# A top-32 cross-attention on one core: the rest rows of two batches share one tile

## The chip, the cores and the metric

The kernel runs on one core of a Trainium2 chip. The metric is the device time of one execution in microseconds (us). A difference under about 0.3% can't be told from none.

## The reference

The input x is 16 batches of 100 rows of 512 numbers, the context 16 batches of 722 rows. One decoder layer is computed: three sublayers, each added to x.

```python
x = x + self_attn(layernorm(x))      # 4 branches of 16 heads, masks by distance, one learned null key per head
x = x + cross_attn(layernorm(x), ctx, ctx)
x = x + real(ifft(fft(layernorm(x)) @ w)) + bias

# cross_attn, 16 heads of 32 dims:
scores = q @ k.T / SCALE                     # 16 x 16 x 100 x 722
top_scores, top_idx = top_k(scores, 32)
w = softmax(top_scores)
out = (w @ take(v, top_idx)) @ Wo.T + bo
```

## The kernel before

It is two programs, one after the other. The first (`self_program`) does the self-attention for all batches and writes its sum to DRAM, the second (`cross_program`) the cross-attention and the feed-forward product. Each loops over the batches, all five engines run one instruction stream each, written out by hand, and semaphores order them. Factors of matrix products are split into a high and a low part and multiplied in three products (`split3`, L86 to L90).

**The second program.** The queries of one batch have 16 heads x 100 rows. Four heads share a group of 32-dimension strips, so a group has 4 x 100 = 400 query rows: three tiles of 128 rows and 16 rows left over. Four groups make 12 full tiles, and the 4 x 16 = 64 rows left over are tile 12, the rest tile (`Tile.rest`). Since its rows belong to four groups, it needs keys and queries gathered from partitions 96 to 127 of each group: `rest_keys` and `rest_queries` (SyncE, L1014 to L1032) copy them with eight and four DMAs into `RKH`, `RKL` and `R32`. `RKH` and `RKL` lie in the memory of `raw`, into which `load_context` loads the next batch's context.

A batch is seven steps (`STEPS`), six with two full tiles and the seventh with the rest tile. For each tile TensorE makes 128 x 722 scores in `pS` (`score`), ScalarE copies them to `S` (`keep_scores`, L1426), and VectorE finds the 32 greatest of each row in four rounds: MAX8 finds eight, MATCH_REPLACE8 replaces them by a very small number in `W` (L1604, L1613, L1621, L1624). It does the rounds of the step's two tiles in turns. ScalarE exponentiates `S` and `W`, GpSimd subtracts (`weights`, L1102), which leaves the weights of the 32 chosen keys, TensorE transposes them (`weights_T`, L1255) and multiplies with the values (`values`, or `rest_values` for the rest tile), ScalarE copies numerators and denominators to `NR`, and GpSimd, or VectorE for the rest rows (L1633), multiplies them into `ctxT`.

The streams are staggered by steps (`tiles_at`): in step s VectorE works on `cur`, TensorE scores the tiles `coming` next and transposes and multiplies the `old` ones of two steps before, ScalarE and GpSimd treat the `last` ones. Three pairs of buffers `S` and two of `W` hold this. Beside it, TensorE projects the keys and values of the next batch in 14 slices, placed by the table `PLAN`: for each step, slices before and after the second scores.

```python
    PLAN = [([12], [13]), ([], [0, 1]), ([2], [3]), ([4, 5], [6]), ([], [7, 8, 9]), ([10], []), ([], [11])]
```

Step 0 in the list is for the batch's own last two slices. Slice 10 is the last key slice. Also in the steps: the next batch's queries in step 1, the last batch's output projection in step 2 (L1348), its feed-forward product in step 5 (L1321). The high part of the queries (`QH`) is made by ScalarE and the low part (`QL`, `query_low`, L1135) by GpSimd in step 5. Each batch's first tile waits for both.

**The first program.** In the stretch before batch 0 the weights stream in through nine buffers in the memory of `E`; ScalarE makes the high parts, VectorE the low parts of 16 pieces (`lows`, L458) and GpSimd those of the 8 value pieces (`v_low`, L302). The null key's rows, one for the weights in `E` and one for the values in `V`, are made in partition 0 and copied by DMA to partition 100 (`nulls`).

## Time and profile before

| | |
|---|---|
| median of 3 runs | 2210.67 us (2207.01 to 2215.05) |
| the profiled execution | 2211.0 us |
| its span in the trace | 2209.2 us |
| first program | about 0 to 680 us |
| second program: first search on VectorE, last | 735.0 us, 2174.5 us |

The page gives for each engine the time in which it was busy. "Idle before" is the time in which an engine stood still ahead of a group of instructions, with the engine and line that ended it. L is a line of the kernel. In the order of time, a line merges neighbours of one kind ("x6"), with the start, the duration of all together and in brackets the idle time ahead. Operations of VectorE overlap somewhat, so a sum of durations is more than the time they take. PEclk is TensorE's granted clock as a share of 2.4 GHz.

### The profile page before, as it was taken

The numbers are of one execution on the slowest core, as the hardware profiler recorded it, in microseconds if no ns is written. First come the engines' busy times: TensorE is split into PE (matmuls) and PEld (weight loads), VectorE is DVE, ScalarE is ACT, GpSimd is POOL, SyncE is SP. The second block draws the span as 40 slices with busy tenths as digits, with TensorE's granted clock in tenths as the row PEclk, the third lists the DMA queues.
The fourth block names the chain that finished last, engine by engine and source line by source line (L and its number), as shares of the span: only waits on it lengthen the run. The fifth ranks groups of instructions, "written<-read, shape, count | busy, mean of one in ns | idle before, by whom it ended". The sixth has DMA issues, their size and how long they took to land.

```text
span 2209.2 us, 50184 instructions
## 1 busy us (share of the span) xinstructions
PE 1969.3 (89%) x19536; PEld 1531.8 (69%) x19536; DVE 1886.3 (85%) x3501; ACT 1325.0 (60%) x2640; POOL 1297.0 (59%) x1566
## 2 busy tenths in 40 slices
PE   4899999999988889999898998998989989899866
PEld 2566666666563778787787777886878777777753
DVE  6667576767644699999999999999999999999993
ACT  4333333333322577877777778787777777777753
POOL 6465565656443356666656656666565666666542
PEclk8899999999988999999999999999999999999976
DMA  6000000000036010111101101111010110110100
GB/s 199 13 16 21 16 16 21 13 24 13 24 143 145 28 36 14 41 31 36 33 21 53 33 21 41 27 40 33 22 53 19 36 39 21 48 33 22 36 1 12
DMA packets 51175, 82.35 MB, mean 37 GB/s; under 512 B 9809, under 2 KB 26465, under 8 KB 50938
## 3 DMA queue, kind: packets, MB, share of 16 engines
q1 hardware_dynamic: 46442, 71.70, 11.1%
q0 software_dynamic: 2736, 4.16, 1.0%
q10 hardware_dynamic: 1760, 3.28, 0.5%
q8 instruction: 155, 2.54, 0.5%
q14 instruction: 82, 0.67, 0.1%
HBM read 60.54 MB, written 9.86 MB: 32 GB/s over the span
## 4 chain that ended last, share of the span: by engine, by line
DVE 44%; PE 10%; issue 9%; ACT 3%; POOL 1%; DMA 1%; POOLq 0%; DVEq 0%; ACTq 0%; another core or an unknown queue 0%
DVE ca_top L1613 19%; DVE ca_W L1624 17%; DVE ca_W L1621 4%; DVE ca_top L1604 3%; PE ca_pF L88 2%; PE ca_pF L89 2%; PE ca_pF L90 2%; DMA x_scratch<-y_scratch 1%; PE ca_pX L1357 1%; ACT ca_W L1409 1%; PE ca_pT L1255 1%; PE ca_pO L1302 1%; PE ca_pS L88 1%; PE ca_pX L1348 1%; POOL ca_S L1102 0%
## 5 line engine op out<-in xcount | busy, mean ns | idle before, releaser
L1624 DVE MATCH_REPLACE8 ca_W<-ca_top,ca_W 128x722 f32<-128x722 f32 (+1 forms) x624 | 555.1, 899 | 0.0
L1613 DVE MAX8 ca_top<-ca_W 128x8 f32<-128x722 f32 (+1 forms) x624 | 538.5, 903 | 1.7
L1102 POOL TENSOR_TENSOR ca_S<-ca_S,ca_W 128x722 f32<-128x722 f32 (+1 forms) x208 | 357.8, 1740 | 104.5 <-ACT ca_W L1409 104.5
L88 PE MATMUL ca_pS<-ca_KH,ca_QH 128*128 128x362 f32 (+1 forms) x384 | 150.5, 392 | 105.7 <-ACT ca_S L1426 97.8
L1080 POOL TENSOR_TENSOR ca_KL<-ca_K,ca_KH 128x384 fp32r<-128x384 f32 (+1 forms) x128 | 123.0, 961 | 200.8 <-ACT ca_KH L1401 198.3
L1419 ACT ACTIVATE ca_S<-ca_S,ca_shift 128x722 f32<-128x722 f32 (+1 forms) x208 | 175.9, 891 | 54.2 <-POOL ca_shift L1094 54.0
L1409 ACT ACTIVATE ca_W<-ca_W,ca_shift 128x722 f32<-128x722 f32 (+1 forms) x208 | 186.5, 897 | 27.4 <-DVE ca_W L1624 27.2
L341 POOL TENSOR_TENSOR sa_ss<-sa_ss,sa_minus_half 100x16 f32<-100x16 f32 x64 | 190.1, 2986 | 21.2 <-DVE sa_ss L528 21.2
L1431 ACT ACTIVATE ca_PT<-ca_pT 128x768 f32<-128x768 f32 (+1 forms) x208 | 163.0, 784 | 65.4 <-PE ca_pT L1255 61.1
L88 PE MATMUL ca_pF<-ca_cH,ca_WkH 128*128 128x338 f32 (+1 forms) x512 | 188.5, 368 | 9.4 <-ACT ca_K L1399 9.4
L1604 DVE MAX8 ca_top<-ca_S 128x8 f32<-128x722 f32 (+1 forms) x208 | 180.0, 903 | 16.6 <-ACT ca_S L1426 16.2
L1426 ACT ACTIVATE ca_S<-ca_pS 128x722 f32<-128x722 f32 (+1 forms) x208 | 159.7, 768 | 56.1 <-PE ca_pS L90 55.7
L1621 DVE MATCH_REPLACE8 ca_W<-ca_top,ca_S 128x722 f32<-128x722 f32 (+1 forms) x208 | 184.8, 897 | 0.0
L1088 POOL TENSOR_TENSOR ca_cL<-ca_raw,ca_cH 128x768 fp32r<-128x768 f32 (+1 forms) x60 | 103.0, 1738 | 137.5 <-ACT ca_cH L1386 137.5
L438 ACT ACTIVATE sa_E<-sa_pq 100x300 f32<-100x300 f32 x256 | 86.5, 426 | 157.9 <-PE sa_pq L90 157.8
L1255 PE MATMUL ca_pT<-ca_ident,ca_S 128*128 128x128 f32 (+1 forms) x1248 | 176.2, 278 | 4.5 <-ACT ca_PT L1431 3.7
L89 PE MATMUL ca_pF<-ca_cL,ca_WkH 128*128 128x338 f32 (+1 forms) x512 | 174.3, 340 | 0.0
L90 PE MATMUL ca_pF<-ca_cH,ca_WkL 128*128 128x338 f32 (+1 forms) x512 | 173.5, 339 | 0.0
L519 DVE TENSOR_TENSOR sa_qk<-sa_pp,sa_bias_qk 100x512 f32<-100x512 f32 x64 | 44.3, 691 | 141.4 <-PE sa_pp L90 141.4
L88 PEld LDWEIGHTS ca_pS<-ca_KH,ca_QH 128*128 128x128 f32 x384 | 76.2, 199 | 125.3 <-ACT ca_S L1426 110.0
L1255 PEld LDWEIGHTS ca_pT<-ca_ident,ca_S 128*128 128x128 f32 (+1 forms) x1248 | 140.3, 144 | 26.4 <-issue 15.7
L330 POOL TENSOR_SCALAR_AFFINE_SELECT sa_E<-sa_E 100x400 f32<-100x400 f32 x256 | 146.9, 574 | 17.9
(223 smaller groups left out, 5142.1 us busy)
## 6 DMA issues: line engine op xcount, KB each, us to landing
ca_raw<-in_ctxT SPq DMA_DIRECT2D x32, 384.0 KB, 3.7
ca_raw<-in_ctxT SPq DMA_DIRECT2D x32, 338.0 KB, 3.1
ca_RKH<-ca_KH SPq DMA_DIRECT2D x64, 90.2 KB, 2.1
ca_RKL<-ca_KL SPq DMA_DIRECT2D x64, 90.2 KB, 2.1
sa_xin<-in_x SPq DMA_DIRECT2D x16, 200.0 KB
sa_xres<-in_x SPq DMA_DIRECT2D x16, 200.0 KB
x_scratch<-sa_x SPq DMA_DIRECT2D x16, 200.0 KB
x_scratch<-y_scratch POOLq DMA_DIRECT2D x16, 200.0 KB, 13.6
```

The source lines that it names most:

```text
L88: pe.matmul(out, ah, bh, start=start, stop=False)
L89: pe.matmul(out, ah, bl, start=False, stop=False)
L90: return pe.matmul(out, al, bh, start=False, stop=stop)
L341: pool.tensor_tensor(part, part, minus_half[:, 0:NH], ALU.pow).then_inc(norm_ready, 1)
L1102: pool.tensor_tensor(S[k][rows, :], S[k][rows, :], W[r][rows, :], ALU.subtract).then_inc(p_ready, 1)
L1255: last = pe.transpose(pT[:, 128 * k:128 * k + t.rows], S[slot(tb, t)][0:t.rows, KEY0[k]:KEY0[k] + 128], ident[0:t.rows, 0:t.rows])
L1409: act.activation(W[r][rows, :], W[r][rows, :], ACT.Exp, bias=shift[rows, r:r + 1], scale=SCALE).then_inc(f_ready, 1)
L1419: act.activation(S[slot(tb, t)][rows, :], S[slot(tb, t)][rows, :], ACT.Exp, bias=shift[rows, r:r + 1], scale=SCALE).then_inc(e_ready, 1)
L1604: dve.max(top[r][rows, 0:8], S[slot(tb, t)][rows, :]).then_inc(peaked, 1)
L1613: n_of[t.i] = order.mark(dve.max(top[r][rows, 8 * k:8 * k + 8], W[r][rows, :]))
L1621: dve.match_replace(W[r][rows, :], eight, S[slot(tb, t)][rows, :], REMOVED).then_inc(removed, 1)
L1624: ins = dve.match_replace(W[r][rows, :], eight, W[r][rows, :], REMOVED)
```

## The change

**The second program.** The rest tiles of batches 2n and 2n+1 become one tile of 128 rows, which is the seventh step of the even batch; an odd batch has six steps. Rows 0 to 63 are the even batch's, 64 to 127 the odd one's. TensorE makes the scores of each half by itself (`score` and `rest_score`, both in step 5 of the even batch), ScalarE copies the second to partitions 64 to 127 of `S`. There is still one pair `RKH`, `RKL`: SyncE copies the odd batch's keys into it once the first half is scored, and the next context load waits for the second half's scores. The gathered queries have two buffers now, and are made a batch ahead. The last key slice of an odd batch is projected in step 4 of the even one (`PAIR_PLAN`). In an odd batch the next batch's query parts are made in step 4 and its first scores come after the feed-forward product (`swap`). The output of the second half goes to `second_rest`, and in the next batch's step 2 ScalarE copies it to `ctxT`.

**The first program.** VectorE makes the low parts of all 24 pieces; `v_low` is gone. The null rows are made in partitions 96 to 100, of which the values overwrite the first four, so the two copies go. GpSimd issues the small loads first and the biases after the first four high parts.

```diff
+            for t, a in SETUP:
+                pool.dma_start(t, a).then_inc(setup_in, 16)
...
-            def v_low(u):
...
+                    need(pool, null_values, n)
+                    pool.tensor_tensor(V[null, n, :], V[null, n, :], null_bias[n], ALU.subtract).then_inc(null_values, 1)
                 pool.wait_ge(null_values, NL)
-                pool.dma_start(V[T:T + 1, :, :].rearrange("p n d -> p (n d)"),
-                               V[0:1, :, :].rearrange("p n d -> p (n d)")).then_inc(null_in, 16)
-                pool.wait_ge(null_weights, 1)
-                pool.dma_start(E[T:T + 1, :, :, :].rearrange("p h n q -> p (h n q)"),
-                               E[0:1, :, :, :].rearrange("p h n q -> p (h n q)")).then_inc(null_in, 16)
...
+                    pool.wait_ge(hi_made, CC)
+                    for t, a in BIAS:
+                        pool.dma_start(t, a).then_inc(bias_in, 16)
+                    nulls()
...
-                    for u in range(QKU, QKU + CC):
-                        v_low(u)
...
                     biased(2)
+                    lows(range(QKU, QKU + 2))
                     squares(2)
+                    biased(3)
+                    lows(range(QKU + 2, QKU + CC))
+                    squares(3)
                     rope(0)
-                    biased(3)
-                    squares(3)
+                    lows(range(QKU + CC, len(UNITS)))
+                    rope(1)
                     statistics(1)
-                    rope(1)
                     summed()
                     rope(2)
                     rope(3)
                     normalised(1)
+                    picks()
                     order.finish()
...
+    RUN = [(b, s) for b in range(B) for s in range(7 - b % 2)]
+    PLACE = [(b, t.i) for b, s in RUN for t in STEPS[s]]
...
+    PAIR_PLAN = [([12], [13]), ([], [0, 1]), ([2], [3]), ([4, 5], [6]), ([7], [8, 9, 10]), ([], []), ([11], [])]
...
+        R32 = [sb(f"R32{p}", [128, 4 * REST]) for p in range(2)]
+        RH, RL = ([sb(f"{n}{p}", [128, 4 * REST], F32R) for p in range(2)] for n in ("RH", "RL"))
...
+        NR = sb("NR", [128, 2, PAIR])
+        second_rest = sb("second_rest", [128, 4 * REST])[3 * DH:128, :]
...
+        def ring(b, t):
+
+            return 2 * (step_of(b, t) % 2) + t.i % 2
...
+            if tiles and s == 6 and b.const % 2:
+                return [], [], [], [], []
+            at = RUN.index((b.const, s)) if tiles else (s - 7 if b.const < 0 else len(RUN) + s)
+
+            def of(n):
+                if not 0 <= n < len(RUN):
+                    return []
+                ob, os = RUN[n]
+                return [(At(ob), ob % 2, t) for t in STEPS[os]]
+
+            return of(at), of(at - 1), of(at - 2), of(at + 1), of(at - 3)
...
+            return (PAIR_PLAN if b.const % 2 else PLAN) if b.const else FIRST_PLAN
...
+            def rest_keys(b, p, after):
+
+                need(sp, s_mm, after)
                 sp.wait_ge(k_hi, b.count(8, 8))
                 sp.wait_ge(k_lo, b.count(8, 8))
-                for to, of in ((RKH, KH[par]), (RKL, KL[par])):
+                for to, of in ((RKH, KH[p]), (RKL, KL[p])):
                     for g in range(4):
-                        sp.dma_start(to[DH * g:DH * g + DH, :].bitcast(F32), of[3 * DH:128, g, :].bitcast(F32)).then_inc(rk_in, 16)
+                        sp.dma_start(to[DH * g:DH * g + DH, :].bitcast(F32),
+                                     of[3 * DH:128, g, :].bitcast(F32)).then_inc(rk_in, 16)
...
+                if tiles and b.const % 2:
+                    rest_keys(b, par, scored(b.next(-1), NT))
+                    sp.wait_ge(s_mm, scored(b, 0))
...
+                    rest_queries(b.next(), 1 - par)
+                if tiles and not b.const % 2:
+                    sp.wait_ge(ctx_hi, b.next().count(4, 4))
+                    sp.wait_ge(ctx_lo, b.next().count(4, 4))
+                    rest_keys(b, par, scored(b, 0))
...
-                    if s == 5 and tiles and nxt:
+                    if s == 5 and tiles and nxt and not b.const % 2:
                         query_low(bn)
                     for x in first + second:
                         if slice_of(x[0], x[2])[1] == "K":
                             key_low(*x)
-                    if s == 2 and tiles:
-                        pool.wait_ge(r_hi, b.count(1, 1))
-                        pool.tensor_tensor(RL[:, :], R32[:, :], RH[:, :].bitcast(F32), ALU.subtract).then_inc(r_lo, 1)
                     if s == 0 and nxt:
                         pool.wait_ge(squares1_ready, bn.count(1, 1))
                         scales(rstd1_ready)
                     if s == 3 and prev:
                         pool.wait_ge(squares2_ready, b.count(1, 0))
                         scales(rstd2_ready)
+                    if s == 4 and nxt:
+                        rest_query_low(bn, pn)
                     if s in (0, 3) and tiles and nxt:
                         for piece in range(2):
                             context_low(bn, 2 * (s // 3) + piece)
+                    if s == 4 and tiles and nxt and b.const % 2:
+                        query_low(bn)
...
+            def rest_score(tb, p, before):
+
+                pe.wait_ge(r_lo, tb.count(1, 1))
+                pe.wait_ge(rk_in, tb.count(128, 128))
+                pe.wait_ge(s_ready, before)
+                for keys, cols in KEYS:
+                    last = split3(pe, pS[0:4 * REST, cols], RH[p][:, :], RL[p][:, :], RKH[:, keys], RKL[:, keys], True, True)
+                last.then_inc(s_mm, 1)
...
+                pe.wait_ge(kv_out, tb.next().count(NSL, NSL))
+                pe.matmul(pO[3 * DH:128, DEN:DEN + PAIR], rZ[:, r:r + 1].broadcast_to((128, DH)), ident[:, :],
                           start=True, stop=True)
-                for g in range(4):
-                    at = NUM + REST * g
-                    for k in range(KC):
-                        last = pe.matmul(pO[3 * DH:128, at:at + REST], V[tp][:, k, 128 * g + 3 * DH:128 * g + 128],
-                                         PT[t.i % 2][:, k, REST * g:REST * g + REST], start=k == 0, stop=k == KC - 1)
+                for p in (tp, 1 - tp):
+                    for g in range(4):
+                        at = 4 * REST * p + REST * g
+                        for k in range(KC):
+                            last = pe.matmul(pO[3 * DH:128, NUM + at:NUM + at + REST],
+                                             V[p][:, k, 128 * g + 3 * DH:128 * g + 128],
+                                             PT[0][:, k, at:at + REST], start=k == 0, stop=k == KC - 1)
...
+                    swap = s == 5 and tiles and b.const % 2
+                    if coming and not swap:
...
+                    if coming and swap:
+                        score(*coming[0])
...
+                    if s == 5 and tiles and not b.const % 2:
+                        rest_score(bn, 1 - par, scored(b, NT))
...
+            def keep_second_rest(tb, tp, t):
+                act.wait_ge(s_mm, scored(tb, NT + 1))
+                act.activation(S[slot(tb, t)][4 * REST:128, :], scores[0:4 * REST, :], ACT.Copy).then_inc(s_ready, 1)
...
+                    if s == 2 and prev and not b.const % 2:
+                        act.wait_ge(ot_ready, b.count(GROUPS, -1))
+                        act.wait_ge(second_ready, b.const // 2)
+                        act.activation(ctxT[3 * DH:128, :, T - REST:T], chunks(second_rest, 4), ACT.Copy).then_inc(ot_ready, 1)
...
+                        dve.max(top[r][:, 0:8], S[slot(tb, t)][:, :]).then_inc(peaked, 1)
...
-                        if k == 3 and s == 1 and prev:
+                        if k == 3 and s == 1 and prev and b.const % 2:
                             dve.wait_ge(ot_ready, b.count(GROUPS, -1))
-                            dve.wait_ge(o_kept, b.count(GROUPS, 0))
-                            rest = [chunks(NR[3 * DH:128, i, 0:4 * REST], 4) for i in range(2)]
-                            dve.tensor_tensor(ctxT[3 * DH:128, :, T - REST:T], rest[0], rest[1],
+                            dve.wait_ge(o_kept, kept(b, 0))
+                            rest = [chunks(NR[3 * DH:128, i, :], 8) for i in range(2)]
+                            dve.tensor_tensor(ctxT[3 * DH:128, :, T - REST:T], rest[0][:, 0:4, :], rest[1][:, 0:4, :],
                                               ALU.mult).then_inc(ot_ready, 1)
+                            dve.tensor_tensor(chunks(second_rest, 4), rest[0][:, 4:8, :], rest[1][:, 4:8, :],
+                                              ALU.mult).then_inc(second_ready, 1)
                         if k == 1 and s == 3 and tiles and not prev:
```

On TensorE, in step 5 of batch 2: the feed-forward product (`ca_M`), the last key slice (`ca_cH`, `ca_WkH`), the rest tile's scores (`ca_RKH`), the transposes (`ca_ident`, `ca_S`). Before:

```order
L88 MATMUL ca_pS<-ca_RKH,ca_RH 64x362 [waits ca_s_ready,ca_rk_in,ca_r_lo]
...
L1321 MATMUL ca_pX<-ca_M,ca_xT 100x512 [waits ca_x2T_ready]
L1321 MATMUL ca_pX<-ca_M,ca_xT 100x512 x3
L1323 MATMUL ca_pX<-ca_x,ca_ident 100x512 [waits ca_x2f_ready]
L88 MATMUL ca_pF<-ca_cH,ca_WkH 128x338 [waits ca_kv_out]
...
L1255 MATMUL ca_pT<-ca_ident,ca_S 128x128 [waits ca_pt_ready,ca_p_ready]
L1255 MATMUL ca_pT<-ca_ident,ca_S 128x128 x5
L1297 MATMUL ca_pO<-ca_ident,ca_rZ 32x100 [waits ca_rz_ready,ca_pt_ready,ca_o_kept]
```

And after:

```order
L88 MATMUL ca_pS<-ca_RKH,ca_RH 64x362 [waits ca_s_ready,ca_rk_in,ca_r_lo]
...
L1352 MATMUL ca_pX<-ca_M,ca_xT 100x512 [waits ca_x2T_ready]
L1352 MATMUL ca_pX<-ca_M,ca_xT 100x512 x3
L1354 MATMUL ca_pX<-ca_x,ca_ident 100x512 [waits ca_x2f_ready]
L1282 MATMUL ca_pT<-ca_ident,ca_S 128x128 [waits ca_pt_ready,ca_p_ready]
L1282 MATMUL ca_pT<-ca_ident,ca_S 128x128 x5
L88 MATMUL ca_pS<-ca_RKH,ca_RH 64x362 [waits ca_s_ready,ca_rk_in,ca_r_lo]
...
L1327 MATMUL ca_pO<-ca_ident,ca_rZ 32x100 [waits ca_rz_ready,ca_pt_ready,ca_o_kept]
```

The key slice is gone from this step, and a second group of scores from gathered keys stands ahead of the values.

On SyncE's queue, from the even batch's keys to the next context load. Before:

```order
L1032 DMA ca_RKH<-ca_KH 32x722 [waits ca_k_hi,ca_k_lo,ca_ctx_lo,ca_ctx_hi]
L1032 DMA ca_RKH<-ca_KH 32x722 x3
L1032 DMA ca_RKL<-ca_KL 32x722 x4
L1044 DMA ca_xin<-x_scratch 100x512 [waits ca_x2T_mm,ca_x1T_mm]
L1020 DMA ca_R<-ca_qT 32x16 [waits ca_q_ready,ca_s_mm,ca_zeroed]
L1020 DMA ca_R<-ca_qT 32x16 x3
L1012 DMA ca_raw<-in_ctxT 128x2x384 [waits ca_ctx_lo,ca_ctx_hi] x2
```

And after:

```order
L1043 DMA ca_RKH<-ca_KH 32x722 [waits ca_k_hi,ca_s_mm,ca_k_lo,ca_ctx_lo,ca_ctx_hi]
L1043 DMA ca_RKH<-ca_KH 32x722 x3
L1043 DMA ca_RKL<-ca_KL 32x722 x4
L1056 DMA ca_xin<-x_scratch 100x512 [waits ca_x2T_mm,ca_x1T_mm]
L1043 DMA ca_RKH<-ca_KH 32x722 [waits ca_k_lo,ca_k_hi,ca_s_mm]
L1043 DMA ca_RKH<-ca_KH 32x722 x3
L1043 DMA ca_RKL<-ca_KL 32x722 x4
L1024 DMA ca_raw<-in_ctxT 128x2x384 [waits ca_ctx_lo,ca_ctx_hi,ca_s_mm]
```

The odd batch's eight copies stand right behind the even one's and the small load of x, behind a wait for scores, and the context load behind them.

## Rows read from the trace of the kernel before

**Rows 1.** The page: busy time of each engine over the span.
```profile
PE 1969.3 (89%) x19536; PEld 1531.8 (69%) x19536; DVE 1886.3 (85%) x3501; ACT 1325.0 (60%) x2640; POOL 1297.0 (59%) x1566
```
**Rows 2.** Who waited for whom, 735 to 2175 us: total, times, longest.
```profile
DVE ca_top L1604 <- ACT ca_S L1426: 16.2, 6, 6.0
```
**Rows 3.** VectorE in order of time: start, duration, line, operation, tiles, count.
```profile
1261.29 1.73 DVE L1604 MAX8 ca_top<-ca_S 128x8 f32<-128x722 f32 x2
...
1274.81 0.92 DVE L1604 MAX8 ca_top<-ca_S 64x8 f32<-64x722 f32 x1
...
1282.54 1.71 DVE L1604 MAX8 ca_top<-ca_S 128x8 f32<-128x722 f32 x2
```
**Rows 4.** VectorE's groups by line: count, busy us, mean ns, idle before.
```profile
L1633 DVE TENSOR_TENSOR ca_ctxT<-ca_NR 32x64 f32<-32x64 f32 x16 | 4.8, 303 | 11.1 <-ACT ca_NR L1445 10.7
```
**Rows 5.** Two batches: us; busy PE, PEld, DVE, ACT, POOL; PEclk; DMA share, GB/s.
```profile
1287.60:1376.90 89.30, 81.18 (x773) 68.44 (x771) 88.93 (x160) 68.02 (x131) 56.84 (x70) 0.98 0.12 33
1376.90:1466.00 89.10, 82.06 (x760) 69.83 (x760) 88.73 (x156) 66.61 (x128) 55.16 (x69) 0.94 0.12 31
```
**Rows 6.** TensorE in order of time, steps 4 and 5 of that batch.
```profile
1251.26 0.43 PE L88 MATMUL ca_pS<-ca_KH,ca_QH 128*128 128x362 f32 x1 [2.12 <-ACT ca_S L1426]
...
1260.93 0.87 PE L1255 MATMUL ca_pT<-ca_ident,ca_S 128*128 128x128 f32 x6
1261.56 0.41 PE L88 MATMUL ca_pS<-ca_RKH,ca_RH 128*64 128x362 f32 x1
...
1262.64 3.60 PE L1321 MATMUL ca_pX<-ca_M,ca_xT 128*100 128x512 f32 x8
1266.07 1.02 PE L1323 MATMUL ca_pX<-ca_x,ca_ident 100*100 100x512 f32 x2
```
**Rows 7.** SyncE's queue in order of time: time to issue the copies of the keys.
```profile
1249.85 2.41 SPq L1032 DMA_DIRECT2D ca_RKH<-ca_KH  x4
1252.31 3.33 SPq L1032 DMA_DIRECT2D ca_RKL<-ca_KL  x4
```
**Rows 8.** The page's DMA issues: count, KB each, median us to landing.
```profile
ca_RKL<-ca_KL SPq DMA_DIRECT2D x64, 90.2 KB, 2.1
```
**Rows 9.** TensorE and ScalarE in order of time, step 2 of that batch.
```profile
1225.40 3.60 PE L1348 MATMUL ca_pX<-ca_WoT,ca_ctxT 128*100 128x512 f32 x8
...
1225.87 0.77 ACT L1426 ACTIVATE ca_S<-ca_pS 128x722 f32<-128x722 f32 x1
```
**Rows 10.** TensorE in order of time, batch 0, behind a gap.
```profile
825.44 0.51 PE L1297 MATMUL ca_pO<-ca_ident,ca_rZ 128*32 128x100 f32 x7 [4.55 <-issue]
...
828.01 1.54 PE L1255 MATMUL ca_pT<-ca_ident,ca_S 128*128 128x128 f32 x6
```
**Rows 11.** GpSimd in order of time: the low part of the next queries.
```profile
1268.92 4.57 POOL L1135 TENSOR_TENSOR ca_QL<-ca_qT,ca_QH 32x400 fp32r<-32x400 f32 x4 [0.23 <-issue]
```
**Rows 12.** TensorE in order of time, batch 0, step 5.
```profile
817.12 0.41 PE L88 MATMUL ca_pS<-ca_RKH,ca_RH 128*64 128x362 f32 x1
```
**Rows 13.** VectorE in order of time, end of batch 0 and start of batch 1.
```profile
825.10 0.90 DVE L1604 MAX8 ca_top<-ca_S 64x8 f32<-64x722 f32 x1
...
835.96 0.91 DVE L1604 MAX8 ca_top<-ca_S 128x8 f32<-128x722 f32 x1 [1.49 <-ACT ca_S L1426]
```
**Rows 14.** The chain that ended last: start, us, what.
```profile
2186.36 6.71 PE ca_pX L1348 x8
```
**Rows 15.** VectorE in order of time, the last search operation.
```profile
2174.53 0.89 DVE L1624 MATCH_REPLACE8 ca_W<-ca_top,ca_W 64x722 f32<-64x722 f32 x1
```
**Rows 16.** GpSimd in order of time, ahead of the first program's batch 0.
```profile
38.61 5.50 POOL L302 TENSOR_TENSOR sa_WvL<-sa_E,sa_WvH 128x512 fp32r<-128x512 f32 x4
```
**Rows 17.** VectorE in order of time, the same stretch.
```profile
33.64 2.99 DVE L528 TENSOR_SCALAR sa_ss<-sa_ss 100x16 f32<-100x16 f32 x1
...
38.56 1.62 DVE L493 TENSOR_TENSOR sa_rq<-sa_qk,sa_cos 100x256 f32<-100x256 f32 x1
...
48.71 0.42 DVE L493 TENSOR_TENSOR sa_rq<-sa_qk,sa_cos 100x256 f32<-100x256 f32 x1
```

370 lines of the change are left out of this document (174 added, 196 removed).

## The prediction

> **What bounds the kernel now.** I read four things in this order: the page's busy line, the list of who waited for whom over the second program (735 to 2175 us), VectorE's order of time for one batch, and TensorE's, SyncE's, ScalarE's and GpSimd's order of time around the same batch. The busy line [rows 1] has TensorE above VectorE, 1969.3 us against 1886.3, and misleads, since it averages two programs. In the second program VectorE stands still only 16.2 us for scores, in 6 places, the longest 6.0 us [rows 2], and all six lie in batch 0 and at the start of batch 1. From there on it works without a gap. So a batch of the second program lasts as long as VectorE's top-32 search in it, and what is taken from VectorE there is taken from the time, until another engine comes too late.
>
> VectorE's starts of the first MAX8 of each step give the steps [rows 3]: a step of two tiles takes 1274.81 - 1261.29 = 13.52 us, the last step with the rest tile alone takes 1282.54 - 1274.81 = 7.73 us. It costs more than half of a pair because with one tile each operation waits for the one before it; that the tile has 64 rows and not 128 makes nothing cheaper. A batch is 6 x 13.52 + 7.73 + 0.30 (the product for the rest rows [rows 4]) = 89.2 us. In two such batches TensorE is busy 81.18 of 89.30 us at a mean granted clock of 0.98 and 82.06 of 89.10 us at 0.94 [rows 5]. That is the reserve that everything below draws on.
>
> **The change, part by part.**
>
> *Eight rest steps go.* Sixteen rest tiles of 64 rows become eight of 128 rows with the same operations over 722 columns. The operations' rows are in partitions, so I take the same 7.73 us for a full tile. Saved: 8 x 7.73 = 61.8 us. Pair of batches: from 178.4 to 170.7 us.
>
> *The products for the rest rows.* Sixteen of them at 0.30 us; now eight places have two operations each. The number stays, so does the time: 0.
>
> *Does TensorE keep up?* Its work per pair of batches stays about what it was, 2 x 81.6 = 163 us (transposes of one rest tile less, the value products of the rest rows the same in number), now in 170.7 us. On average it fits. The last key slice of the next batch, moved in every second batch a step earlier, costs four groups of three products, some 1.9 us. It goes to the step where TensorE now stands 2.12 us because the scores' bank is not yet emptied [rows 6], so I cost the move at nothing; with that cover gone it would be 1.9 us of a reserve, not of the path.
>
> *The gathered keys of the second batch.* This is the new wait. One buffer holds the gathered keys. Step 5 of an even batch scores the first half of the rest tile (start 1261.56, next operation 1262.64, which is 1.35 us after VectorE's step start 1261.29 [rows 3, 6]); only then may the copies of the second batch's keys go out, and TensorE waits for them before the second half. The eight copies take 2.41 + 3.33 = 5.7 us to issue [rows 7] and 2.1 us from issue to landing [rows 8], 7.8 us. The feed-forward product in between covers 4.5 us of it (1262.64 to 1267.09 [rows 6]). In the time of step 5: keys there at 1.35 + 7.8 = 9.2 us, scores 1.1 us, copy to SBUF 0.9 us: 11.2 us against the 13.52 us at which VectorE wants the tile. So 2.3 us are left, before what comes next is taken off.
>
> *The output projection of an even batch* now needs a product of GpSimd and a copy of ScalarE that follows the emptying of the second scores. That emptying starts at 1225.87 and takes 0.77 us, while the projection starts at 1225.40 [rows 9]. So TensorE stops 1.2 to 1.5 us there in every second batch. What is queued behind it are a key slice, the values and the next scores. I carry 1.4 us of lateness into step 5; the 2.3 us shrink to 0.9.
>
> *The clock.* Between the feed-forward product with its transposes and the landing TensorE would now be idle some 3 us. The trace has a gap of 2.12 us after which the products run as fast as before (0.43 us for the first, as 0.41 us without a gap [rows 6]), and one of 4.55 us after which six transposes take 1.54 us, where the six at 1260.93 took 0.87: the lower of the two levels, 1.2 GHz [rows 6, 10]. Mine lies between them. At the full clock 0.9 us are left; at half clock the scores take 1.1 us more and VectorE waits 0.2 us. The Trainium skill (TensorE: Matmul & The Clock Gate, section Part 1: The HAM clock gate) says that an idle array falls back to half rate and only work releases it, which speaks against this change; by it the value product behind the wait would be slow too in each even batch. The trace agrees for the long gap and not for the short one.
>
> *Odd batches.* They lose their short last step, so the next batch's first scores must be ready 7.7 us sooner. They need the low part of the queries, 4.57 us on GpSimd [rows 11], which the change puts one step earlier, ahead of the sum that the feed-forward product waits for; TensorE stops about 2 us there. Counted on, the second scores are in SBUF about 12.5 us into the step of 13.52: 1 us left.
>
> Both places have a margin of about 1 us, and the clock moves by more than that from batch to batch [rows 5]. So some pairs wait. I take 0.7 us for each of the seven later pairs, +5 us; bounds 0 and 2 us per pair, 0 to 14 us.
>
> *Batch 0.* There TensorE runs late: the first half is scored from 817.12 and VectorE takes the rest tile at 825.10 [rows 12, 13]. Keys would be there at 818.2 + 7.8 = 826.0, the tile 2 to 3 us later, so VectorE waits about 3.6 us. But batch 1 now starts late as well, its second tile at 835.96 after a wait [rows 13], and that wait goes. Net +1.3 us, bounds 0 and +4.
>
> *The end.* Batch 15 has no rest tile. Now the last projection starts at 2186.36, 10.9 us after VectorE's last search operation ended at 2175.42 [rows 14, 15]. After the change the last thing is a pair, two exponentials, two subtractions, then GpSimd's product and ScalarE's copy: I take 12 us. +1 us, bounds -1 and +3.
>
> *The first program.* Eight subtractions of weights go from GpSimd to VectorE. While GpSimd does them (5.50 us for four, from 38.61 [rows 16]), VectorE's two-input products take 1.62 us instead of 0.42 and a small scaling takes 2.99 us [rows 17]. Eight such products and that scaling carry some 8 x 1.05 + 2.8 = 11.2 us too much. VectorE gets 8 x 0.62 = 5.0 us of work, 1.3 of them in a wait that it has anyway, and loses a wait of 0.7 for a product sum: -11.2 + 3.7 - 0.7 = -8.2 us. The biases now load after the first weights; the first bias addition can come 2 us later. I take -6.5 us, bounds -9 and 0. The null rows in place take two copies out of a chain that ends with this stretch; I give it nothing of its own. The Trainium skill (SBUF — State Buffer, section SBUF: two separate sides) calls the pair of ports that both engines use an exclusive lock, which the 1.62 against 0.42 us bears out; by it the three null products, now beside VectorE's subtractions, could hold those up.
>
> **The sum.** -61.8 + 5 + 1.3 + 1 - 6.5 = -61.0 us. The profiled execution took 2211.0 us (span 2209.2), 0.3 us above the median of the three runs, 2210.67. Forecast: 2210.67 - 61.0 = 2150 us. With all good ends -61.8 + 0 + 0 - 1 - 9 = -72 gives 2139, with all bad ends -61.8 + 14 + 4 + 3 + 0 = -41 gives 2170.
>
> **The rivals.**
>
> *A. TensorE's chain takes over in the odd batches.* An odd batch needs 81.7 us of VectorE and has 81.6 us of TensorE, which also has stops that no other work fills (the two of 1.4 and 2 us above and the one for the keys). If the lateness is not made up in the even batch, an odd batch lasts about 85.7 us, 4 us more: 8 x 4 = 32 instead of my 5 us, 2177 us. For it: the margins of 1 us. Against: the even batch has 89 us for the same work. 18 in 100.
>
> *B. The copies of the keys come one after the other* (slower than before). If each is issued only when the one before has landed, eight take 8 x (0.7 + 2.1) = 22 us. The tile is then ready at 1.35 + 1.4 + 22 + 2 = 27 us instead of 13.5: 13.3 us x 8 = 107 us, and -61.0 - 6.3 + 107 = +40, 2250 us. It begins to cost above 8.7 us of gathering and makes the kernel slower from about 18 us. Against: issues of 0.6 to 0.8 us in a row [rows 7]. 2 in 100.
>
> *C. Nothing waits*, and the first program gives what it can: 2139 to 2145. VectorE shows no gap after batch 1 today, in spite of clocks between 0.94 and 1.00. 14 in 100.
>
> *D. The first and the last part eat it up, or the pairing does not shorten VectorE's list.* VectorE's list of instructions is 60 rows shorter and shows a single 128-row tile in every thirteenth step, so the last is excluded; for an unknown loss I leave 3 in 100, at 2190 and above, a third of it beyond 2217.
>
> **The numbers.** Forecast 63, A 18, C 14, B 2, D 3. A measurement of this kernel tells about 0.3% from no change, 6.6 us. Forecast, A and C all lie below 2204: faster 0.96, same 0.01, slower 0.03. The range for 8 in 10 takes the forecast and C whole and a part of A: 2139 to 2172; 2150 is the likeliest.
>
> **What would show it.** Each step right: VectorE has 200 tiles in the second program instead of 208 and starts two batches 170.7 us apart; one short step of 7.7 us per pair; waits of VectorE for scores at the rest tile below 1 us; the first batch of the first program ready some 6 us sooner. Wrong: waits before the first MAX8 of the rest tile of 2 us and more (A or B, told apart by whether TensorE's second rest scores wait for a DMA), pairs of 175 us and more (A), or a 128-row rest step clearly above 7.73 us.

## Result, and the profile after

The changed kernel takes 2196.78 us (median of 4 runs, 2192.28 to 2197.32) beside 2212.86 us for the kernel before on the same chip: ratio 0.9927, 95% interval 0.9902 to 0.9952. It is 16 us faster, not 61, and lies above the range of 2139 to 2172 us. The profiled execution took 2197.32 us, its span 2195.5 us, against a span of 2209.2 us before. The times below are from the fast runs alone: a run of the kernel before at 2301 us and one of e8 at 5239 us are left out.

The busy line of the page has the same order as before [rows 1], with less on every engine:

```profile
PE 1952.2 (89%) x19472; PEld 1518.1 (69%) x19472; DVE 1822.8 (83%) x3413; ACT 1302.9 (59%) x2600; POOL 1269.3 (58%) x1533
```

VectorE has 1886.3 - 1822.8 = 63.5 us less to do in both programs together, so its work went as promised. That the time did not follow is told by the list of who waited for whom; in total us, number and longest. First VectorE's waits for scores in SBUF (L1461 keeps a tile's scores, L1465 those of the second batch's half of the rest tile):

```profile
DVE ca_top L1665 <- ACT ca_S L1461: 56.6, 27, 6.0
...
DVE ca_top L1665 <- ACT ca_S L1465: 16.6, 8, 2.5
```

Then TensorE's waits in the same list:

```profile
PE ca_pX L1354 <- POOL ca_x L1198: 18.1, 7, 2.6
PE ca_pS L88 <- DMA ca_RKL<-ca_KL: 17.6, 8, 5.7
PE ca_pF L88 <- POOL ca_cL L1104: 12.7, 8, 1.6
PE ca_pX L1381 <- ACT ca_ctxT L1560: 11.7, 8, 1.5
```

16.2 us of waits for scores [rows 2] became 56.6 + 16.6 = 73.2 us, 57 us more: nearly all of the 61.8 us taken from the search. The chain that ended last says the same. Its line on the page before has VectorE first:

```profile
DVE 44%; PE 10%; issue 9%; ACT 3%; POOL 1%; DMA 1%; POOLq 0%; DVEq 0%; ACTq 0%; another core or an unknown queue 0%
```

After, TensorE has taken that place:

```profile
PE 39%; ACT 12%; POOL 7%; issue 6%; DVE 3%; DMA 1%; POOLq 1%; SPq 1%; ACTq 0%; another core or an unknown queue 0%; DVEq 0%
```

VectorE in order of time gives the lengths. The first row is the first search operation, the others are starts of the rest tile of batches 0, 2, 4 and 14, and, behind the first of them, the start of the next step:

```profile
722.96 0.91 DVE L1665 MAX8 ca_top<-ca_S 128x8 f32<-128x722 f32 x1 [5.97 <-ACT ca_S L1461]
...
815.43 0.91 DVE L1665 MAX8 ca_top<-ca_S 128x8 f32<-128x722 f32 x1 [2.30 <-ACT ca_S L1465]
...
823.21 0.90 DVE L1665 MAX8 ca_top<-ca_S 128x8 f32<-128x722 f32 x1
...
996.85 0.91 DVE L1665 MAX8 ca_top<-ca_S 128x8 f32<-128x722 f32 x1 [1.95 <-ACT ca_S L1465]
...
1175.99 0.91 DVE L1665 MAX8 ca_top<-ca_S 128x8 f32<-128x722 f32 x1 [1.99 <-ACT ca_S L1465]
...
2070.36 0.91 DVE L1665 MAX8 ca_top<-ca_S 128x8 f32<-128x722 f32 x1 [1.95 <-ACT ca_S L1465]
```

The rest step of 128 rows takes 823.21 - 815.43 = 7.78 us (7.73 for 64 rows [rows 3]). Seven pairs take 2070.36 - 815.43 = 1254.9 us, 179.3 each, where 170.7 was expected (a pair runs from the rest tile of one even batch to that of the next). The kernel before had its first MAX8 at 734.97 and the rest tile of batch 14 at 2078.38. That cuts the spans into four stretches:

| stretch | before | after | difference | in the prediction |
|---|---|---|---|---|
| start to first MAX8 | 735.0 | 723.0 | -12.0 | -6.5 |
| to the rest tile of batch 0 | 90.1 | 92.5 | +2.3 | part of +1.3 |
| seven pairs | 1253.3 | 1254.9 | +1.7 | 7 x (-7.73 + 0.7) = -49 |
| the rest | 130.8 | 125.1 | -5.7 | -7.7 + 1 |

The difference of the spans is -13.7 us. The whole loss sits in the pairs. From the rest tile of batch 6 to that of batch 8 VectorE waits at three places: at both tiles of batch 8's step 0, at the second tile of its step 4, and at the rest tile. VectorE in order of time:

```profile
1444.48 0.91 DVE L1665 MAX8 ca_top<-ca_S 128x8 f32<-128x722 f32 x1 [2.06 <-ACT ca_S L1461]
1446.65 0.91 DVE L1665 MAX8 ca_top<-ca_S 128x8 f32<-128x722 f32 x1 [1.26 <-ACT ca_S L1461]
...
1504.50 0.92 DVE L1665 MAX8 ca_top<-ca_S 128x8 f32<-128x722 f32 x1 [3.62 <-ACT ca_S L1461]
...
1532.79 0.91 DVE L1665 MAX8 ca_top<-ca_S 128x8 f32<-128x722 f32 x1 [1.95 <-ACT ca_S L1465]
```

That is 8.9 us in one pair. In front of them TensorE stops, which in order of time reads so:

```profile
1438.00 1.10 PE L1354 MATMUL ca_pX<-ca_x,ca_ident 100*100 100x512 f32 x2 [2.59 <-POOL ca_x L1198]
...
1439.97 0.49 PE L90 MATMUL ca_pF<-ca_cH,ca_WkL 128*128 128x338 f32 x1
...
1467.16 0.67 PE L88 MATMUL ca_pS<-ca_KH,ca_QH 128*128 128x362 f32 x1 [2.13 <-ACT ca_S L1461]
1467.62 0.50 PE L89 MATMUL ca_pS<-ca_KL,ca_QH 128*128 128x362 f32 x1
...
1486.48 1.07 PE L1381 MATMUL ca_pX<-ca_WoT,ca_ctxT 128*100 128x512 f32 x2 [1.50 <-ACT ca_ctxT L1560]
...
1511.01 0.42 PE L88 MATMUL ca_pF<-ca_cH,ca_WkH 128*128 128x338 f32 x1 [1.59 <-POOL ca_cL L1104]
...
1522.86 0.41 PE L88 MATMUL ca_pS<-ca_RKH,ca_RH 128*64 128x362 f32 x1
...
1530.71 0.35 PE L88 MATMUL ca_pS<-ca_RKH,ca_RH 128*64 128x362 f32 x1 [1.67 <-DMA ca_RKL<-ca_KL]
```

The first stop is the feed-forward product waiting for GpSimd's sum, the second the second score tile of a step waiting until the first is out of PSUM, the third the output projection waiting for the second batch's rest context, the fourth a key slice waiting for the context's low part, the fifth the gathered keys. Behind the first two, the products of 338 and 362 columns take 0.49 and 0.50 us where they take 0.32 and 0.33 elsewhere: the granted clock there is 0.50, the lower of the two levels, 1.2 GHz, for some 3 us each time. Two more stops of the pair lie in the odd batch (2.12 us for a kept score tile, 1.65 us for kept keys); in the kernel without waits below they are still there.

### The profile page after: what moved, and what is told of

It reads as the page before. It is cut to its first block, busy times and chain, and to the rows that moved or that the text cites. A ratio compares the mean times of both kernels' runs of the same rounds, so it can differ in the third digit from the quotient of the medians.

```text
span 2195.5 us, 49817 instructions
## 1 busy us (share of the span) xinstructions
PE 1952.2 (89%) x19472; PEld 1518.1 (69%) x19472; DVE 1822.8 (83%) x3413; ACT 1302.9 (59%) x2600; POOL 1269.3 (58%) x1533
## 4 chain that ended last, share of the span: by engine, by line
PE 39%; ACT 12%; POOL 7%; issue 6%; DVE 3%; DMA 1%; POOLq 1%; SPq 1%; ACTq 0%; another core or an unknown queue 0%; DVEq 0%
PE ca_pF L88 6%; PE ca_pF L90 6%; PE ca_pF L89 6%; PE ca_pO L1332 3%; PE ca_pT L1282 3%; ACT ca_W L1443 3%; PE ca_pX L1390 3%; PE ca_pX L1381 3%; PE ca_pS L88 2%; POOL ca_QL L1151 2%; PE ca_pS L89 2%; PE ca_pS L90 2%; ACT ca_S L1461 2%; ACT ca_S L1453 1%; ACT ca_top L1446 1%
## 5 line engine op out<-in xcount | busy, mean ns | idle before, releaser
L1684 DVE MATCH_REPLACE8 ca_W<-ca_top,ca_W 128x722 f32<-128x722 f32 x600 | 535.8, 906 | 0.0
L1674 DVE MAX8 ca_top<-ca_W 128x8 f32<-128x722 f32 x600 | 518.7, 909 | 0.8
L1117 POOL TENSOR_TENSOR ca_S<-ca_S,ca_W 128x722 f32<-128x722 f32 x200 | 344.8, 1746 | 101.6 <-ACT ca_W L1443 101.6
L1665 DVE MAX8 ca_top<-ca_S 128x8 f32<-128x722 f32 x200 | 175.6, 911 | 73.4 <-ACT ca_S L1461 56.6
L88 PE MATMUL ca_pF<-ca_cH,ca_WkH 128*128 128x338 f32 (+1 forms) x512 | 190.1, 371 | 22.9 <-POOL ca_cL L1104 12.7
L1470 ACT ACTIVATE ca_PT<-ca_pT 128x768 f32<-128x768 f32 x200 | 161.6, 808 | 56.0 <-PE ca_pT L1282 52.7
L1453 ACT ACTIVATE ca_S<-ca_S,ca_shift 128x722 f32<-128x722 f32 x200 | 169.2, 894 | 36.1 <-POOL ca_shift L1110 35.8
L1443 ACT ACTIVATE ca_W<-ca_W,ca_shift 128x722 f32<-128x722 f32 x200 | 179.8, 899 | 15.0 <-DVE ca_W L1684 15.0
L1282 PE MATMUL ca_pT<-ca_ident,ca_S 128*128 128x128 f32 x1200 | 170.4, 278 | 10.8 <-ACT ca_PT L1470 10.2
L1681 DVE MATCH_REPLACE8 ca_W<-ca_top,ca_S 128x722 f32<-128x722 f32 x200 | 178.3, 903 | 0.0
L89 PE MATMUL ca_pF<-ca_cL,ca_WkH 128*128 128x338 f32 (+1 forms) x512 | 176.5, 345 | 0.0
L1461 ACT ACTIVATE ca_S<-ca_pS 128x722 f32<-128x722 f32 (+1 forms) x200 | 154.1, 771 | 36.8 <-PE ca_pS L90 36.6
L88 PE MATMUL ca_pF<-ca_WvH,ca_cH 128*128 128x512 f32 x384 | 151.5, 395 | 0.0
```

The source lines that it names most:

```text
L88: pe.matmul(out, ah, bh, start=start, stop=False)
L89: pe.matmul(out, ah, bl, start=False, stop=False)
L1117: pool.tensor_tensor(S[k][:, :], S[k][:, :], W[r][:, :], ALU.subtract).then_inc(p_ready, 1)
L1282: last = pe.transpose(pT[:, 128 * k:128 * k + 128], S[slot(tb, t)][:, KEY0[k]:KEY0[k] + 128], ident[:, :])
L1443: act.activation(W[r][:, :], W[r][:, :], ACT.Exp, bias=shift[:, r:r + 1], scale=SCALE).then_inc(f_ready, 1)
L1453: act.activation(S[k][:, :], S[k][:, :], ACT.Exp, bias=shift[:, r:r + 1], scale=SCALE).then_inc(e_ready, 1)
```

## Experiments

**One half of the change at a time.** Both kernels are put together from the two files: the first program of one, the second program of the other.

> The first program of the change (null rows made in place, low parts of the V weights on VectorE) with the second program of the kernel before. The traces put 12.0 us of the change's gain ahead of the first MAX8 of the search (734.97 to 722.96 us) and 1.7 us behind it. If the two programs are independent, this kernel is 12 us faster than before (2201 us, ratio 0.9946) and its first MAX8 stands at 723 us. Rival: part of the 12 us comes from the second program's own set-up, which this kernel has as before; then it is 4 to 8 us faster.

> The second program of the change with the first program of the kernel before. Theory (TensorE's chain now sets the length of a pair of batches, and waits of about 9.6 us a pair took the place of the 7.7 us that the search was shortened by): within 4 us of before, 2209 to 2213 us. Rival (the second program gains by itself and the two parts disturb each other): more than 8 us faster.

Measured: the first program alone 2199.95 us (ratio 0.9948, 0.9932 to 0.9964), some 11.5 us faster, as expected. Its first MAX8 stands at 725.24 us, not at 723: over the eleven traces with the new first program that start lies between 719.4 and 727.6 us, over the three with the old one between 732.3 and 737.6, so a single trace gives this part only to a few us. The second alone 2202.24 us (0.9955, 0.9941 to 0.9969), some 9.5 us faster: below what the theory expected, and in the rival's range. The two gains sum to 21 us, the change gave 16, with an interval of 5.5 us to either side, so that the parts disturb each other isn't shown. The second program's code is that of the change, but its seven pairs take 178.1 us on average (175.8 to 180.2) where the profiled run of the change has 179.3 (176.4 to 181.4). A pair bound by TensorE's chain has no fixed length; those bound by VectorE had one to 0.2 us in the last five pairs of the kernel before (178.52 to 178.74).

**The sum before the low queries.** In the odd batches GpSimd does, in the change, first this and then that:

```profile
1432.05 4.55 POOL L1151 TENSOR_TENSOR ca_QL<-ca_qT,ca_QH 32x400 fp32r<-32x400 f32 x4 [0.22 <-issue]
1436.68 1.27 POOL L1198 TENSOR_TENSOR ca_x<-ca_x,ca_bias_f 100x512 f32<-100x512 f32 x1
```

```diff
-                    if s == 4 and tiles and nxt and b.const % 2:
-                        query_low(bn)
                     if s == 4 and prev:
                         pool.wait_ge(xn2_ready, b.count(1, 0))
                         pool.tensor_tensor(x2[:, :], x2[:, :], bias_f[:, :], ALU.add).then_inc(x2f_ready, 1)
+                    if s == 4 and tiles and nxt and b.const % 2:
+                        query_low(bn)
```

> The change, with one order turned round on GpSimd in the odd batches: the sum x2 + bias (1.27 us) before the low parts of the queries (4.57 us), not behind. Theory: the feed-forward product then no longer waits 2.59 us for the sum, and the two waits at the start of the even batch (2.06 to 2.52 and 1.26 us) go; 7 pairs by 2.5 to 3.3 us, so 2174 to 2180 us against 2197 of the change. Rival A (TensorE's later backlog takes it back: its next wait, 3.6 us at the second tile of step 4, grows by the same amount): within 5 us of the change. Rival B (the low parts, 1.3 us later, now hold up the next scores): the gain is only 1 us a pair.

Measured: 2164.05 us (0.9793, 0.9770 to 0.9815), some 30 us below the change, more than expected; the pairs take 174.2 to 176.1 us. VectorE's waits in the trace of this kernel:

```profile
DVE ca_top L1665 <- ACT ca_S L1461: 27.9, 14, 6.0
...
DVE ca_top L1665 <- ACT ca_S L1465: 16.5, 8, 2.5
```

The waits at step 0 are gone in all pairs and those at step 4, 2.2 to 4.0 us in the change, are 0.6 to 2.9: TensorE's lateness at step 4 was in part inherited from step 0. The waits at the rest tile did not move.

**The rest tile sooner.** SyncE let the four copies of the high keys go at `k_hi`, and those of the low keys at `k_lo`; TensorE scored the first half behind the last key slice of step 4; ScalarE kept it before the high queries, and GpSimd made the low part of the rest queries in step 3, not 4. The diff shows the copies and the scores.

```diff
-                sp.wait_ge(k_hi, b.count(8, 8))
-                sp.wait_ge(k_lo, b.count(8, 8))
-                for to, of in ((RKH, KH[p]), (RKL, KL[p])):
+                for to, of, made in ((RKH, KH[p], k_hi), (RKL, KL[p], k_lo)):
+                    sp.wait_ge(made, b.count(8, 8))
...
+                    if s == 4 and tiles and not b.const % 2:
+                        rest_score(b, par, scored(b, NT - 1))
```

> The change, with the first half of the rest tile scored behind the last keys of step 4 instead of in step 5, kept before the next batch's high queries, and the four copies of the high keys let go when the high keys are there (1521.70 in the trace of the change), not with the low ones. Theory: the second half's keys land 2.4 us sooner, so the wait of 1.95 to 2.50 us ahead of the rest tile goes to 0 to 0.5: 8 times 2 us, 2181 us against 2197. Rival (the time only moves to the start of the next batch, since TensorE has the same work and the next batch's scores follow its chain): VectorE's wait at the rest tile is gone but the pair stays at 179 us, 2194 to 2198 us.

Measured: 2202.79 us (median of seven runs, 2191.86 to 2208.82; ratio 0.9956, 0.9933 to 0.9978), no better than the change. The trace is of the fastest of them. In it the wait at the rest tile fell to 1.0 to 1.5 us, and 1.4 to 4.2 us came up at the second tile of the next step, where TensorE now waited for the low queries. GpSimd in order of time:

```profile
1525.36 4.55 POOL L1150 TENSOR_TENSOR ca_QL<-ca_qT,ca_QH 32x400 fp32r<-32x400 f32 x4 [0.22 <-issue]
```

TensorE in order of time:

```profile
1529.96 0.44 PE L88 MATMUL ca_pS<-ca_KH,ca_QH 128*128 128x362 f32 x1 [2.39 <-POOL ca_QL L1150]
```

The rival held: the wait moved. (The time lies some us above the rival's 2194 to 2198.) Two more kernels went this way.

> The two orders of e3 and e8 together, and the next batch's high and low queries made a step sooner in the even batches as well, since in e8 VectorE's wait at the rest tile fell from about 2.1 to 1.0 us but 1.9 to 4.1 us came up at the next tile, behind the low queries on GpSimd. Theory (each place is a wait of TensorE or VectorE with a cause of its own): the pair goes from 174.9 us in e3 to 171 to 173, and the kernel to 2142 to 2152 us. Rival (TensorE's work sets the pair at about 175): within 4 us of e3, 2160 to 2166.

> e9, and two more orders on ScalarE: the second batch's rest context is copied before the keys of step 2 are kept (TensorE waited 1.50 us for it ahead of the output projection), and the first score tile of even steps 1 and 3 is kept before the exponentials of the picked ones. Theory: what is left at step 4 of the even batch (up to 3.8 us in e3) goes too, so 1 to 3 us a pair less than e9, 2128 to 2145 us, close to the 2139 us at which nothing waits. Rival: TensorE has too much work in the even batch's steps 0 to 4 for any order to help, and it comes out as e9.

Measured: 2191.06 us (0.9901, 0.9877 to 0.9926) and 2164.70 us (0.9776, 0.9753 to 0.9799). Both missed their theory and their rival: e9 is some 25 us slower than the sum's order alone, with waits of 2.5 to 5.6 us at the rest tile. The even batch's step 4 got the high queries (2.20 us of ScalarE) and the low ones (4.55 us of GpSimd) ahead of work for the rest tile. I did not take these changes apart, so which of them costs it stays open.

**Two orders on ScalarE instead.** The first moves the copy of the second batch's rest context ahead of the keys of step 2; the second keeps the first score tile in step 1 of the even batch before the exponentials of the picked ones (2.2 us), not after. In the diff the four lines of the copy are shown only at their new place; they stood behind the keeping of the second score tile.

```diff
+                    early_keep = s == 1 and prev and not b.const % 2
+                    if coming and early_keep:
+                        keep_scores(*coming[0])
                     for x in last:
                         exps_left(*x)
...
-                    if coming and not swap:
+                    if coming and not swap and not early_keep:
                         keep_scores(*coming[0])
...
+                    if s == 2 and prev and not b.const % 2:
+                        act.wait_ge(ot_ready, b.count(GROUPS, -1))
+                        act.wait_ge(second_ready, b.const // 2)
+                        act.activation(ctxT[3 * DH:128, :, T - REST:T], chunks(second_rest, 4), ACT.Copy).then_inc(ot_ready, 1)
                     for x in slices(s, 0, b, par, tiles, nxt):
                         keep(*x)
```

> e3 and the two orders on ScalarE (early copy of the rest context; in even batches the first score tile of step 1's turn kept before the exponentials of the picked ones), without anything at the rest tile. It tells the backlog at step 4 from the copies of keys: theory 1 to 3 us a pair less than e3's 174.9, 2142 to 2156 us; the wait of 2 us at the rest tile stays. Rival: as e3, 2164.

Measured, with the sum first as well: **2139.61 us** (0.9667, 0.9649 to 0.9686), 57 us below the change and 73 below the kernel before. This is the fastest version, below the 2142 to 2156 us expected. VectorE's waits in it:

```profile
DVE ca_top L1668 <- ACT ca_S L1461: 14.6, 5, 6.0
...
DVE ca_top L1668 <- ACT ca_S L1465: 2.3, 1, 2.3
```

Two rest tiles, VectorE in order of time:

```profile
1331.31 0.90 DVE L1668 MAX8 ca_top<-ca_S 128x8 f32<-128x722 f32 x1
...
1501.97 0.89 DVE L1668 MAX8 ca_top<-ca_S 128x8 f32<-128x722 f32 x1
```

All waits that are left lie in batch 0 and at the start of batch 1. A pair takes 170.66 us (170.64 to 170.66 behind the first). VectorE leads the chain that ended last again:

```profile
DVE 47%; issue 9%; PE 8%; ACT 2%; DMA 1%; POOL 1%; SPq 0%; DVEq 0%; ACTq 0%; another core or an unknown queue 0%; POOLq 0%
```

Nothing was changed at the rest tile, and its wait is gone too, against the expectation. TensorE in order of time in this kernel, step 5 of batch 8:

```profile
1489.49 0.41 PE L88 MATMUL ca_pS<-ca_RKH,ca_RH 128*64 128x362 f32 x1
...
1497.34 0.35 PE L88 MATMUL ca_pS<-ca_RKH,ca_RH 128*64 128x362 f32 x1 [1.67 <-DMA ca_RKL<-ca_KL]
```

From the first half to the second it is 7.85 us, as in the change (1522.86 to 1530.71), with the same stop of 1.67 us. Only now the first half comes 1.05 us behind VectorE's step start (1488.44), not 5.6 us (1517.22 in the change). So the keys come in time. Nor are all of TensorE's stops gone: the gathered keys still cost it 1.67 us a pair, the context's low part 1.6, and in the odd batch it waits at least as long as in the change for the kept scores and keys:

```profile
1395.95 0.43 PE L88 MATMUL ca_pS<-ca_KH,ca_QH 128*128 128x362 f32 x1 [2.50 <-ACT ca_S L1461]
...
1403.09 0.43 PE L88 MATMUL ca_pF<-ca_cH,ca_WkH 128*128 128x338 f32 x1 [2.12 <-ACT ca_K L1434]
```

The products behind both run at full speed, and the pair loses nothing by them.

**Is it TensorE's work or its stops?** The values' projection without one of its products:

```diff
-                        last = split3(pe, pF[:, n % 2, :], cH[:, c, keys], cL[:, c, keys],
-                                      WvH[:, c, :], WvL[:, c, :], c == 0, c == CC - 1)
+                        pe.matmul(pF[:, n % 2, :], cH[:, c, keys], WvH[:, c, :], start=c == 0, stop=False)
+                        last = pe.matmul(pF[:, n % 2, :], cL[:, c, keys], WvH[:, c, :], start=False, stop=c == CC - 1)
```

> The change, with the values' projection computed from two of its three products (the context by the low part of the weights is left out); nothing else is touched. It takes 12 slices of 4 matmuls of 0.228 us, 10.9 us a pair, from TensorE alone. Theory (TensorE's chain sets the pair): the waits of VectorE at the even batch's steps 0 and 4 shrink and the pair falls from 179 to 171 to 174 us, the kernel to 2140 to 2160 us. Rival (VectorE, ScalarE or GpSimd set it, or the waits hang on GpSimd and the DMAs alone): less than 1 us a pair, above 2189 us.

Measured: 2169.82 us (0.9804, 0.9777 to 0.9830), pairs of 175.0 to 177.3 us, 176.5 on average. 10.9 us of work less shortens the pair by 2.8 us; no work less, but three orders turned round, shortens it by 8.6. So my theory that TensorE's work sets the pair fell in the main: less work wins back a third of the loss, the three orders all of it. The windows of one pair each (columns as in [rows 5]) show it. The change:

```profile
1352.42:1442.60 90.18, 82.61 (x788) 70.44 (x782) 89.43 (x158) 65.89 (x128) 56.67 (x69) 0.95 0.11 33
1442.60:1532.79 90.19, 81.19 (x773) 68.21 (x772) 81.48 (x144) 67.09 (x131) 53.91 (x70) 0.98 0.13 32
```

The kernel with less work:

```profile
1340.67:1429.10 88.43, 77.65 (x752) 65.57 (x746) 88.06 (x156) 66.13 (x130) 57.50 (x72) 0.96 0.12 34
1429.10:1517.89 88.79, 77.44 (x741) 65.42 (x741) 82.51 (x147) 66.23 (x129) 53.21 (x67) 0.94 0.13 33
```

The kernel with three orders turned round:

```profile
1501.97:1590.00 88.03, 81.75 (x821) 69.36 (x820) 87.66 (x157) 66.78 (x130) 56.40 (x70) 1.00 0.09 26
1590.00:1672.62 82.62, 76.12 (x713) 63.54 (x711) 82.62 (x148) 66.00 (x129) 54.79 (x68) 1.00 0.16 43
```

TensorE is busy 163.8 us in the first, 155.1 in the second and 157.9 in the third. The third does the same matmuls as the first in 5.9 us less, at a clock of 1.00. The pairs shown of the first and the third are among their dear and cheap ones: over all seven pairs the means are 162.6, 155.6 and 159.2 us, so the clock is worth 3.4 us a pair on average.

**Each of the three orders taken out of the best version.**

> e11 without the early keeping of scores: the sum ahead of the low queries, and the early copy of the rest context. Of the 4.2 us a pair that e11 gained on e3 (174.9 to 170.7) TensorE's stop ahead of the output projection is 1.5 us, and the wait for kept scores 2.1 us with half clock behind it. Theory (each order takes its own stop away, and only together they bring the rest tile in time): pair 172 to 174 us, 2149 to 2160 us. Rival (one of the two does it all): either 2140 here and e3's 2164 in e14, or the reverse.

> e11 without the early copy of the rest context: the sum ahead of the low queries, and scores kept early. Theory: pair 171.5 to 173.5 us, 2145 to 2157 us, a little better than e13 since its stop is the longer one. Rival as for e13.

> e11 without the sum ahead of the low queries: only the two orders on ScalarE. Theory: the feed-forward product's wait of 2.6 us and VectorE's waits at the even batch's step 0 stay, those at step 4 shrink; pair 174 to 176 us, 2164 to 2178 us. Rival (the backlog over steps 0 to 4 was the root, and the wait for the sum only its result): pair below 172 us, 2145 us or less.

| kernel | us | ratio, 95% interval | pairs, us |
|---|---|---|---|
| all three (e11) | 2139.61 | 0.9667, 0.9649 to 0.9686 | 170.6 to 170.7 after the first |
| without keeping early (e13) | 2157.48 | 0.9759, 0.9732 to 0.9786 | 172.4 to 177.0 |
| without copying early (e14) | 2148.04 | 0.9713, 0.9695 to 0.9732 | 171.2 to 173.0 |
| without the sum first (e15) | 2159.13 | 0.9763, 0.9738 to 0.9788 | 173.0 to 174.6 |

Each order is worth 8 to 20 us and none does it alone; e13 and e14 are as expected, e15 is some 5 us below its 2164 to 2178. In each trace the stop whose order was left as it was is there, 2.12 us in e13, 1.50 in e14 and 2.58 in e15, and the other two are gone.

**The best version with the first program of before.**

> e11 with the first program of the kernel before. It says what the second program's change is worth by itself once TensorE keeps up: with pairs of 170.7 us 7.7 x 8 = 62 us less than before, less 2 to 4 us for batch 0: 2151 to 2155 us, 12 us above e11. Rival (the parts do not add): differs from e11 by less than 6 or more than 16 us.

Measured: 2152.18 us (0.9732, 0.9711 to 0.9753), 12.6 us above e11, as expected: here the two programs add. With TensorE in time, the second program's part of the change, with the three orders, is worth 60 us, against some 9.5 us as it stands.

## Why the prediction was wrong

*Right.* The rest step goes and costs the same with 128 rows (7.78 against 7.73 us). VectorE without waits has pairs of 170.66 us; 170.7 was predicted. The three stops that the prediction names came, at about their size: "about 2 us" for the feed-forward product (2.59), 1.2 to 1.5 at the output projection (1.50), and the gathered keys, which took 6.8 us from the first half being scored (1523.93) to the second half's start (1530.71), where 7.8 was put. The copies do not go one by one (rival B). The last part cost 2.0 us (+1, up to 3), batch 0 +2.3 up to its rest tile, inside the bound of 4. One sign misled: TensorE's second rest scores do wait for a DMA (1.67 us), by which the prediction meant to tell B from A, though what came late was the first half.

*The step that failed* is the one behind "I take 0.7 us for each of the seven later pairs". Measured, 1254.9 - 7 x 170.66 = 60.3 us, 8.6 us a pair, where the bounds reached 2. (Before, the seven pairs took 1253.3 us, 4.5 more than the 7 x 178.4 reckoned with.) It was reached in three wrong ways:
- The two places were sized one by one, each for a TensorE that is in step with VectorE a step earlier, and only 1.4 us of lateness was carried over. In the trace TensorE has the first half scored not 1.35 + 1.4 = 2.75 but 6.7 us behind VectorE's step start (its start is 5.6 us behind, where 0.27 + 1.4 = 1.7 was carried). e3 shows the inheritance: mending a stop in the odd batch also shrank the wait at step 4 of the next one.
- Two stops were not counted: the second score tile that waits for ScalarE to keep the first (2.13 us; e13, which leaves that order as it was, is 18 us above e11) and the last key slices in step 4, which wait for the context's low part. I had costed the moved key slice at nothing, because it went into the gap of 2.12 us; in the change eight waits for the low part, 12.7 us, stand there. They are still there in e11, 1.6 us each, while its pairs are as short as VectorE allows: by themselves they cost nothing. What they add beside the other stops was not tried.
- "On average it fits", 163 us in 170.7, was right and no protection: 7.7 us of reserve in a pair stand against stops of 2.6, 2.1, 1.5, 1.6 and 1.7 us, before any of them costs clock. Taking away the first three is enough.

*The clock.* I let a stop of some 2 us cost nothing, from one gap of 2.12 us with full speed behind it [rows 6]. The same trace has the same gap at the same place of another batch with half clock behind it (granted clock 0.50):

```profile
1431.08 0.49 PE L88 MATMUL ca_pS<-ca_KH,ca_QH 128*128 128x362 f32 x1 [2.12 <-ACT ca_S L1426]
1431.37 0.50 PE L89 MATMUL ca_pS<-ca_KL,ca_QH 128*128 128x362 f32 x1
```

In the change the stop of 2.12 to 2.13 us ahead of the second scores of an even batch's step 1 has half clock right behind it in three of seven pairs. But the stops of 2.50 us in e11 have full speed behind them, all four. So from its length alone no stop between 2.1 and 2.6 us can be costed, and the clock costs 3.4 us of TensorE's time a pair on average. The Trainium skill (TensorE: Matmul & The Clock Gate, section Part 1: The HAM clock gate) says that the gate is throttled by default and that activity releases it. The stops with half clock behind them agree, those of 2.50 us don't show it; the sum should have carried it as a chance at every stop, not for the long gap alone.

*Rival A* named the right mechanism, TensorE's chain taking over, and its sign, pairs of 175 us and more, came. Its price, 4 us a pair, was half of the 8.6 measured, because it let the odd batch alone lose time and left out the clock. 18 in 100 was too little: two places with margins of 1 us each had to be right together.

*The first program* gave 12.0 us in the traces, some 11.5 in e1, not 6.5, and the path was another one. VectorE's list in this stretch did shrink about as reckoned: its last operation there that both kernels have, the normalisation of batch 1, starts at 51.49 us, before at 59.43, 7.9 us sooner against 8.2 (the later biases cost nothing: the first bias addition starts at 21.37 us in the change and 21.16 before). But what ScalarE, and behind it TensorE, stood still for was the null rows' copy, whose removal I gave "nothing of its own". The kernel before, ScalarE and TensorE in order of time:

```profile
58.48 1.08 ACT L402 ACTIVATE sa_V<-sa_pp 100x512 f32<-100x512 f32 x2 [7.46 <-DMA sa_E<-sa_E]
...
59.71 0.90 PE L662 MATMUL sa_pp<-sa_ident,sa_rq 100*128 100x100 f32 x4 [9.66 <-ACT sa_V L402]
```

And after:

```profile
46.43 1.09 ACT L388 ACTIVATE sa_V<-sa_pp 100x512 f32<-100x512 f32 x2
...
47.66 0.53 PE L653 MATMUL sa_pp<-sa_ident,sa_rq 100*128 100x100 f32 x4 [2.72 <-ACT sa_V L388]
```

ScalarE keeps the values 58.48 - 46.43 = 12.05 us sooner, which is the whole gain. So the term put at nothing was on the path. GpSimd made the null rows behind its low parts of the weights, so the work moved off GpSimd can have brought them sooner as well as the copies left out; no run parts the two. The null products were held up beside VectorE's subtractions, as was feared: 3.52 and 4.10 us, and 1.29 for the third.

## What to carry over

When the bounding engine is relieved in a place where the next one is busy for 95% of the new period (163 of 170.7 us), add up all stops of that second engine along one whole period and carry its lateness from step to step; a margin worked out for one step from a fresh start is no margin. And look at the order of the queues before the amount of work: three operations moved within their own engines' queues gained 57 us, while 8 x 10.9 = 87 us of TensorE's work taken away gained 27.

## What the runs showed of the hardware

A stop of TensorE can cost twice, its length and half clock behind it, and at 2.1 to 2.6 us its length doesn't tell whether it will. The 2.12 us stops had either level behind them, in one and the same kernel; stops of 2.50 us had full clock. With three stops of 2.59, 2.13 and 1.50 us taken out of the pair, the same matmuls took 159.2 us instead of 162.6 on average, and the granted clock went from 0.95 to 0.99 up to 0.98 to 1.00. With 10.9 us of work gone but the stops left, the clock was 0.94 or 0.95 in every pair, and only 7.0 us of busy time went. The kernel bound by VectorE (e11) repeats its pairs to 0.1 us from the second on; the change, bound by TensorE's chain, varies by 5 us from pair to pair with the same code, e12 and e3 by 2.
